# Graph attention of chunk 0 woven into the last attention iterations, and the first recurrence half step mixed with the last output products

## The chip, the cores and the metric

One core of one Trainium2 chip runs the whole program. The metric is the device time of one execution in microseconds (us). The engines are named as in the profile: PE (TensorE matmuls, with PEld its weight loads), DVE (VectorE), ACT (ScalarE), POOL (GpSimd) and SP (SyncE, which issues DMAs). Work passes between engines through semaphores; every engine runs its own instructions in program order.

## The reference

Four blocks follow each other on x of shape (128, 64, 256), each applied to h = relu(layernorm(x)) and added to x. The adjacency matrix (64 x 64) is the same for all 128 graphs.

```python
# block 0: masked attention, 8 heads of 32;  block 1 the same, then o + layernorm(o)*gamma + beta
scores = einsum('bqhd,bkhd->bhqk', q, k) / sqrt(HD);  attn = softmax(scores masked by adj)
out = einsum('bhqk,bkhd->bqhd', attn, v) @ Wo + bo
# block 2: graph attention
h = x @ W
e = leaky_relu(h@a1 [:, :, None] + h@a2 [:, None, :], 0.2) * mask
h_prime = einsum('bij,bjf->bif', softmax(e), h)
return elu(h_prime + beta * h)
# block 3: gated recurrence, T = 3 steps (the first factors of av are the adjacency products)
for _ in range(T):
    a_in = a_out = adj @ h;  av = concat([a_in, a_out])
    z = sigmoid(av@w3 + h@u3);  r = sigmoid(av@w4 + h@u3)
    hv = tanh(av@w5 + (r*h)@u5);  h = (1-z)*h + z*hv
```

## The kernel before, in words

x stays in SBUF for the whole program: 64 tiles of 128 rows, worked on as 16 chunks of 4 tiles (512 rows, 8 graphs). PSUM is two groups of four banks: `ring` and `scores` (also called `high`).

The two attention blocks are one software pipeline of 32 steps (T = 32; chunk c of block 0 is step c, chunk c of block 1 is step 16 + c). Iteration i does the scores and softmax of step i, the transposes and value products of step i-1, the output products of step i-2 and, in block 1, the normalisation of the output (steps i-3 and i-4), and it prepares q, k and v of step i+1. `iterations` runs the bodies: a few written out, a hardware loop of two bodies per turn, more written out, a second loop of five turns (iterations 20 to 29), and iteration 30. Iteration 31 and the drain of the pipeline are written out by hand after it, differently for each engine. Every float32 product is three products of split high and low parts (`product`, line 99), so PE runs most of the time on line 99.

Chunk 0 and chunk 1 of blocks 2 and 3 start in that hand written stretch. A chunk's graph attention is a serial chain over all engines: row statistics (DVE `rows_stats`), `norm` (POOL), `graph_normalise` (ACT), `graph_rows` (PE transposes), `graph_high` (ACT) and `graph_low` (DVE), four `graph_product` (PE) with `copy_hw` (ACT), `graph_s2` (PE), `graph_scores` (DVE), `g_shift` (POOL), `g_exponential` (ACT), `graph_attention` (DVE), `graph_attT` (PE), `copy_attT` (DVE), `graph_aggregate` (PE), and then `graph_out` on ACT and DVE, which adds to x. After it `recurrence_stats`, `norm`, `norm_rows` and `enter` bring the chunk into the recurrence.

The recurrence is a chain of half steps: two chunks are in flight, each half step does one step of one of them, and graph attention of the next two chunks runs inside them. `begin` is half step 0 of chunk 0; half step 1 (chunk 1) opens on DVE with r times h, line 1368, whose low part lets PE start the u5 products. From there on PE hardly waits. The order on each engine is that in which the code is written; there is no planner. One rule of the drain matters below: `o_normalise` of chunk c writes one of two buffers `o_n`, so it waits until `final_sum` of chunk c-2 has read it; `scale` (POOL) waits for it, and `final_sum` of c for `scale`.

## Time and profile before

| what | us |
|---|---|
| median of 3 runs | 1505.97 (1505.79 to 1506.27) |
| the profiled execution, its own time | 1503.79 |
| its span, first to last instruction | 1502.0 |
| PE, DVE, ACT, POOL busy in the span | 1464.7, 1246.0, 990.1, 536.0 |
| iterations 20 to 30 of the pipeline | about 369.6 to 562.6 in the span |
| iteration 31, drain and half step 0, up to PE's u5 products of half step 1 | 562.6 to 634.9 |

The busy share of PE is close to full over the whole program, except in the last of these stretches, where the granted clock is also lower for a time. PE's pipelined matmuls overlap, so PE counts as busy where it is only nearly so; start times of equal pieces of two iterations say more than the busy share.

### The profile page before, as it was taken

How to read it: one execution, taken by the hardware profiler on the slowest of the kernel's cores; microseconds unless marked ns; L12 is line 12 of the kernel's file. 1: busy time of each engine (PE TensorE's matmuls, PEld its weight loads, DVE VectorE, ACT ScalarE, POOL GpSimd, SP SyncE). 2: the span in 40 equal slices, each digit the busy share in tenths (PEclk: the TensorE clock that was granted, in tenths of full speed). 3: DMA queues.
4: the chain of work that ended last, by engine and by line, in shares of the span. 5: the costliest groups of instructions: out<-in, count | busy, mean ns of one | idle time of the engine just before them, and what ended most of it. 6: DMA issues, size and time to landing. Idle time of an engine off the chain costs nothing.

```text
span 1502.0 us, 45862 instructions
## 1 busy us (share of the span) xinstructions
PE 1464.7 (98%) x18922; PEld 1237.3 (82%) x18922; DVE 1246.0 (83%) x2518; ACT 990.1 (66%) x1795; POOL 536.0 (36%) x622
## 2 busy tenths in 40 slices
PE   8999999899999998799999999999999999999997
PEld 7898999799888887688888888888887887887886
DVE  4888877989999998888888888888888888888767
ACT  5767767567777776666666666666666666666564
POOL 3876776667888886411101101101111111111000
PEclk9999999999999999899999999999999999999999
DMA  8200000002333334100000000000000000000000
GB/s 268 87 2 0 0 0 2 16 17 45 60 68 68 58 57 59 29 1 1 29 1 2 30 1 1 30 1 1 30 1 1 30 1 1 29 2 1 29 2 28
DMA packets 36839, 40.89 MB, mean 27 GB/s; under 512 B 11872, under 2 KB 31840, under 8 KB 36704
## 3 DMA queue, kind: packets, MB, share of 16 engines
q0 software_dynamic: 4608, 16.78, 5.9%
q1 hardware_dynamic: 32096, 22.10, 4.9%
q8 instruction: 111, 1.82, 0.5%
q14 instruction: 24, 0.20, 0.0%
HBM read 13.71 MB, written 8.39 MB: 15 GB/s over the span
## 4 chain that ended last, share of the span: by engine, by line
PE 78%; DVE 11%; POOL 5%; issue 4%; ACT 1%; DMA 0%; POOLq 0%; DVEq 0%; SPq 0%; ACTq 0%
PE ring L99 34%; PE scores L99 28%; PE scores L1705 3%; DVE total L1040 2%; PE ring L1505 2%; PE ring L1774 2%; PE scores L1469 2%; POOL s L543 2%; PE ring L1545 1%; DVE stats L1012 1%; POOL rstd L534 1%; PE ring L1689 1%; PE ring L1846 1%; DVE oT_lo L1058 1%; PE ring L1647 1%
## 5 line engine op out<-in xcount | busy, mean ns | idle before, releaser
L543 POOL TENSOR_TENSOR s<-s,mx 128x512 f32<-128x512 f32 x128 | 138.3, 1103 | 56.0 <-DVE mx L1036 55.8
L549 POOL TENSOR_TENSOR s<-s,rtotal 128x512 f32<-128x512 f32 x128 | 131.8, 1067 | 31.8 <-DVE rtotal L1042 31.5
L613 POOL TENSOR_TENSOR r_var_eps<-r_mean_var,eps 128x4 f32<-128x4 f32 x16 | 8.1, 509 | 377.3 <-DVE r_mean_var L1207 377.3
L697 ACT ACTIVATE s<-s 128x512 f32<-128x512 f32 x128 | 77.9, 642 | 69.5 <-POOL s L543 69.5
L1370 DVE TENSOR_TENSOR rhp_lo<-r,rhp_hi 128x1024 fp32r<-128x1024 f32 x47 | 57.6, 1225 | 73.5 <-ACT rhp_hi L912 73.5
L1031 DVE SCALAR_TENSOR_TENSOR s<-scores,mask 128x512 f32<-128x512 f32 x128 | 87.1, 680 | 30.5 <-PE scores L1469 30.5
L877 ACT ACTIVATE r<-r,bias_half 128x512 f32<-128x512 f32 x96 | 64.3, 717 | 58.9 <-DVE r L1341 58.9
L931 ACT ACTIVATE hv<-scores,bias 128x512 f32<-128x512 f32 x94 | 64.7, 688 | 55.1 <-PE scores L99 55.1
L905 ACT ACTIVATE later_w<-ring 128x512 f32<-128x512 f32 x64 | 34.8, 596 | 99.1 <-PE ring L1774 99.1
L709 ACT ACTIVATE pT<-ring 128x512 f32<-128x512 f32 x128 | 66.1, 603 | 42.4 <-PE ring L1505 42.4
L1036 DVE TENSOR_REDUCE mx<-s 128x8 f32<-128x512 f32 x128 | 87.8, 686 | 4.4
L1332 DVE TENSOR_TENSOR agg_lo<-scores,agg_hi 128x512 fp32r<-128x512 f32 x96 | 61.8, 685 | 32.6 <-ACT agg_hi L870 32.2
L1040 DVE TENSOR_REDUCE total<-s 128x8 f32<-128x512 f32 x128 | 82.5, 645 | 0.0
L99 PE MATMUL ring<-agg_hi,w4T_hi 128*128 128x512 f32 x192 | 78.2, 407 | 2.3 <-DVE agg_lo L1332 2.3
L99 PE MATMUL scores<-rhp_hi,u5T_hi 128*128 128x512 f32 (+1 forms) x192 | 80.3, 418 | 0.0
L99 PE MATMUL scores<-agg_hi,w5T_hi 128*128 128x512 f32 (+1 forms) x192 | 78.3, 408 | 0.0
L99 PE MATMUL scores<-agg_hi,w3T_hi 128*128 128x512 f32 x192 | 77.2, 402 | 0.0
L613 POOL TENSOR_TENSOR g_var_eps<-g_mean_var,eps 128x4 f32<-128x4 f32 x16 | 8.3, 520 | 191.9 <-DVE g_mean_var L1207 191.9
L99 PE MATMUL scores<-agg_hi,w3T_lo 128*128 128x512 f32 x192 | 75.8, 395 | 0.0
L99 PE MATMUL scores<-agg_lo,w3T_hi 128*128 128x512 f32 x192 | 75.8, 395 | 0.0
L99 PE MATMUL ring<-agg_hi,w4T_lo 128*128 128x512 f32 x192 | 75.8, 395 | 0.0
L99 PE MATMUL ring<-agg_lo,w4T_hi 128*128 128x512 f32 x192 | 75.7, 394 | 0.0
(314 smaller groups left out, 5128.2 us busy)
## 6 DMA issues: line engine op xcount, KB each, us to landing
x<-beta_less_one POOLq DMA_DIRECT2D x16, 512.0 KB, 4.7
x<-o POOLq DMA_DIRECT2D x16, 512.0 KB, 6.6
out_x<-x SPq DMA_DIRECT2D x15, 512.0 KB, 2.9
x<-in_x SPq DMA_DIRECT2D x1, 6144.0 KB, 25.5
later_w<-in_L_gnn_w_w SPq DMA_DIRECT2D x3, 512.0 KB, 5.5
x<-in_x SPq DMA_DIRECT2D x2, 512.0 KB, 5.4
x<-in_x SPq DMA_DIRECT2D x1, 1024.0 KB, 7.0
stage<-in_L_gnn_w_qkv SPq DMA_DIRECT2D x3, 256.0 KB, 3.2
```

What stands on the lines that cost most here:

```text
L99: last = pe.matmul(out, s, m, start=(begins and n == 0), stop=(ends and n == len(terms) - 1))
L543: pool.tensor_tensor(sr, sr, mx[:, r, :].unsqueeze(2).to_broadcast([P, CT * 2, N]), ALU.subtract).then_inc(s_shifted, 1)
L549: pool.tensor_tensor(sr, sr, rtotal[:, r, :].unsqueeze(2).to_broadcast([P, CT * 2, N]), ALU.mult).then_inc(p_ready, 1)
L697: act.activation(s[:, par, r, :, :, :], s[:, par, r, :, :, :], ACT.Exp).then_inc(p_exp, 1)
L709: act.activation(pT[:, r, :, :].rearrange("p t q -> p (t q)"), ring[:, r, :], ACT.Copy).then_inc(pT_copied, 1)
L877: act.activation(r[:, m, :], r[:, m, :], ACT.Tanh, bias=bias_half[:, 1, m:m + 1], scale=0.5)\
L931: act.activation(hv[:, m, :], high[:, 2 + m, :], ACT.Tanh, bias=bias[:, 2, m:m + 1])\
L1031: dve.scalar_tensor_tensor(sr(par, r), scores[:, r, :].rearrange("p (a k) -> p a k", k=N), SCALE, masks[layer_of(i, lay)][:].unsqueeze(1). ...
L1036: dve.reduce_max(mx[:, r, :], sr(par, r), AX.X).then_inc(s_max, 1)
L1040: dve.reduce_sum(total[:, r, :], sr(par, r), AX.X).then_inc(p_total, 1)
L1332: dve.tensor_tensor(agg.lo[:].rearrange("p m (t g q) -> p g m t q", t=CT, g=2)[:, g], high[:, g, :].rearrange("p (m t q) -> p m t q", m=FT ...
L1370: dve.tensor_tensor(rhp.lo[:], r[:], f32(rhp.hi[:]), ALU.subtract).then_inc(rh_lo_ready, 1)
```

## The change

The second hardware loop is written out (iterations 20 to 30), since its bodies now differ. Chunk 0's graph attention is taken out of the hand written stretch and put into iterations 20 (WEAVE) to 30, a link or two in each, through functions `woven` and `woven_last` that each engine's body calls: statistics at the end of iteration 20, `norm` 21, `graph_normalise` 22, transposes and high and low parts 23, products 24 and 25, s2, sums and maximum 26, exponential 27, attention and its transposes 28, aggregation and the output to x 29, and the statistics for the recurrence 30. Chunk 1's statistics move one iteration earlier. The drain then holds chunk 1's graph attention, `enter` of chunk 0 and `begin`, in which the u3 products of chunk 0, the output products, the values, and the first adjacency products alternate. `o_normalise` and `final_sum` of the last chunks, and the last two `o_stats`, move into `begin`, behind the recurrence's own instructions. Chunk 0 gets buffers of its own; other buffers move to free the room (w_ext's place is taken by chunk 0's hw, then by its recurrence rows).

```diff
+    WEAVE = CHUNKS + 4
...
-            with eng.Fori(0, (CHUNKS - 6) // 2) as j:
-                body(j * 2 + CHUNKS + 4, 0, 1)
-                body(j * 2 + CHUNKS + 5, 1, 1)
-            body(T - 2, 0, 1)
+            for i in range(CHUNKS + 4, T - 1):
+                body(i, i % 2, 1)
...
                     if isinstance(i, int) and i == T - 2:
-                        norm(gn, 0, 0)
...
+                    if isinstance(i, int) and i == WEAVE + 1:
+                        norm(gn, 0, 0)
+                    if isinstance(i, int) and i == WEAVE + 6:
+                        g_shift(0)
...
                 scale(T - 1, 1, 1)
                 norms(T, 0, 1)
-                norm(rn, 0, 0)
-                g_shift(1)
                 scale(T, 0, 1)
+                norm(gn, 2, 0)
+                norm(rn, 1, 1)
+                o_to_x(T + 1, 1, 1)
                 norms(T + 1, 1, 1)
-                o_to_x(T + 1, 1, 1)
+                o_to_x(T + 2, 0, 1)
                 norms(T + 2, 0, 1)
-                o_to_x(T + 2, 0, 1)
-                norm(rn, 1, 1)
                 scale(T + 1, 1, 1)
                 scale(T + 2, 0, 1)
-                group(0)
+                norm(gn, 3, 1)
+                g_shift(2)
+                norm(rn, 2, 0)
+                g_shift(3)
+                norm(rn, 3, 1)
                 with pool.Fori(1, GROUPS - 1) as g:
...
+                def woven(i):
+                    if i == WEAVE + 3:
+                        graph_high(0, high)
+                    if i == WEAVE + 4:
+                        copy_hw(0, 0, high, 2)
+                        copy_hw(0, 1, high, 2)
+                    if i == WEAVE + 5:
+                        copy_hw(0, 2, high, 2)
+                        copy_hw(0, 3, high, 2)
+                    if i == WEAVE + 9:
+                        graph_read(0, high, 2)
+                def woven_last(i):
+                    if i == WEAVE + 2:
+                        graph_normalise(0, 0)
+                    if i == WEAVE + 7:
+                        g_exponential(0)
+                    if i == WEAVE + 9:
+                        graph_exp(0)
...
                 def begin(s):
                     for m in range(FT):
                         act.wait_ge(hu_ready, m + 1)
-                        act.activation(hu[:, m, :], ring[:, 2 + m, :], ACT.Copy).then_inc(hu_copied, 1)
-                    graph_read(1, ring, 0)
+                        act.activation(hu[:, m, :], high[:, m, :], ACT.Copy).then_inc(hu_copied, 1)
+                    g_exponential(1)
+                    o_normalise(T - 1, 1, 1)
+                    o_high(T - 1)
                     agg_high(0)
-                    graph_exp(1)
-                    o_normalise(T + 1, 1, 1)
-                    o_normalise(T + 2, 0, 1)
+                    graph_out(1, high, 2)
+                    o_normalise(T, 0, 1)
                     act.wait_ge(b_ready, 5)
                     r_tanh(0)
                     norm_rows(rn, r_hn[1], 1, 1)
                     enter(1, 1)
                     graph_normalise(2, 0)
+                    o_normalise(T + 1, 1, 1)
+                    o_normalise(T + 2, 0, 1)
...
                 act.wait_ge(xT_ready, T * FT)
-                graph_normalise(0, 0)
+                graph_normalise(1, 1)
                 copy_pT(T - 1)
-                o_normalise(T - 1, 1, 1)
-                graph_high(0, high)
+                norm_rows(rn, r_hn_first, 0, 0)
+                graph_high(1, high)
                 for q in range(R - 1):
                     exponential(T - 1, 1, q)
                 o_high(T - 2)
                 exponential(T - 1, 1, R - 1)
-                for t in range(CT):
-                    copy_hw(0, t, high, 2)
-                graph_normalise(1, 1)
+                copy_hw(1, 0, high, 2)
+                copy_hw(1, 1, high, 2)
+                enter(0, 0, high, 0)
+                copy_hw(1, 2, high, 2)
+                copy_hw(1, 3, high, 2)
                 copy_pT(T)
-                graph_high(1, high)
-                g_exponential(0)
-                o_high(T - 1)
-                copy_hw(1, 0, high, 0, hw_next)
-                copy_hw(1, 1, high, 0, hw_next)
-                graph_out(0, high, 2)
-                copy_hw(1, 2, high, 0, hw_next)
-                copy_hw(1, 3, high, 0, hw_next)
-                o_normalise(T, 0, 1)
-                norm_rows(rn, r_hn[0], 0, 0)
-                g_exponential(1)
-                enter(0, 0, high)
                 halves(act, half)
...
+                def woven(i):
+                    if i == WEAVE + 3:
+                        graph_low(0, high)
+                    if i == WEAVE + 6:
+                        graph_sum(0, high, 0)
+                    if i == WEAVE + 8:
+                        dve.wait_ge(beta_ident_ready, 1)
+                        copy_attT(0, high, 0)
+                    if i == WEAVE + 9:
+                        graph_positive(0, high, 2)
+                def woven_last(i):
+                    if i == WEAVE:
+                        dve.tensor_scalar(beta_ident[:], ident[:], g_beta[:, 0:1], None, ALU.mult)\
+                            .then_inc(beta_ident_ready, 1)
+                        rows_stats(gn, 0, x_final)
+                    if i == WEAVE + 6:
+                        graph_leaky(0)
+                    if i == WEAVE + 7:
+                        dve.memset(first_rows.att[:], 0.0).then_inc(first_att_cleared, 1)
+                    if i == WEAVE + 9:
+                        graph_negative(0)
+                    if i == WEAVE + 10:
+                        recurrence_stats(0)
...
                     if isinstance(i, int) and i == T - 2:
-                        rows_stats(gn, 0, x_final)
+                        rows_stats(gn, 1, x_final)
...
+                    if isinstance(i, int) and i == WEAVE + 8:
+                        graph_attention(0)
...
                 def begin(s):
-                    graph_positive(1, ring, 0)
+                    rows_stats(gn, 2)
+                    graph_positive(1, high, 2)
                     agg_low(0)
                     graph_negative(1)
                     recurrence_stats(1)
+                    take_first(T + 1, 1, 1)
+                    take_out(T - 1, 1, 1, 1)
                     r_sum(0)
+                    o_stats(T, 0, 1)
                     z_sum(0)
-                    rows_stats(gn, 2)
+                    dve.wait_ge(o_stats_ready, CHUNKS - 1)
+                    o_stats(T + 1, 1, 1)
+                    enter(1, 1)
+                    final_sum(T, 0, 1)
+                    final_sum(T + 1, 1, 1)
                     final_sum(T + 2, 0, 1)
-                    enter(1, 1)
...
-                rows_stats(gn, 1, x_final)
                 for q in range(3):
...
                 mask_and_max(T - 1, 1, 3, 1)
...
-                dve.tensor_scalar(beta_ident[:], ident[:], g_beta[:, 0:1], None, ALU.mult).then_inc(beta_ident_ready, 1)
-                graph_scores(0, high, 2)
+                enter(0, 0, high, 0)
+                graph_scores(1, high, 2)
                 final_sum(T - 1, 1, 1)
                 o_stats(T - 1, 1, 1)
                 dve.wait_ge(att_cleared, 1)
-                graph_attention(0)
-                graph_low(1, high)
-                dve.wait_ge(beta_ident_ready, 1)
-                copy_attT(0, high, 2)
+                graph_attention(1)
                 take_first(T, 0, 1)
                 take_out(T - 2, 1, 0, 1)
+                copy_attT(1, high, 2)
                 o_low(T - 1)
-                graph_out(0, high, 2)
-                recurrence_stats(0)
-                graph_scores(1, high, 0, hw_next)
-                o_stats(T, 0, 1)
-                take_first(T + 1, 1, 1)
-                take_out(T - 1, 1, 1, 1)
-                graph_attention(1)
...
+                def woven(i):
+                    if i == WEAVE + 3:
+                        pe.wait_ge(s_masked, i * R + 2)
+                        graph_rows(0, high)
+                    if i == WEAVE + 4:
+                        pe.wait_ge(gw_lo_ready, 1)
+                        pe.wait_ge(s_masked, (i + 1) * R)
+                        graph_product(0, 0, high, 2)
+                        graph_product(0, 1, high, 2)
+                    if i == WEAVE + 5:
+                        pe.wait_ge(s_masked, (i + 1) * R)
+                        graph_product(0, 2, high, 2)
+                        graph_product(0, 3, high, 2)
+                    if i == WEAVE + 6:
+                        pe.wait_ge(s_masked, i * R + 2)
+                        graph_s2(0, high, 0)
+                    if i == WEAVE + 8:
+                        pe.wait_ge(s_masked, i * R + 1)
+                        graph_attT(0, high, 0)
+                    if i == WEAVE + 9:
+                        pe.wait_ge(s_masked, (i + 1) * R)
+                        graph_aggregate(0, high, 2)
...
                 def begin(s):
                     pe.wait_ge(h0_lo_ready, FT)
-                    pe.wait_ge(x_done, T * 2)
                     for m in range(FT):
-                        product(pe, ring[:, 2 + m, :], columns(wT["u3"], m), moving(hp[0])).then_inc(hu_ready, 1)
-                    graph_aggregate(1, ring, 0, hw_next)
-                    pe.wait_ge(e_sum, 2)
-                    pe.wait_ge(hw_copied, 2 * FT)
+                        product(pe, high[:, m, :], columns(wT["u3"], m), moving(hp[0])).then_inc(hu_ready, 1)
+                    o_products(T, 1)
+                    graph_attT(1, high, 2)
+                    values(T, 0)
+                    pe.wait_ge(hu_copied, FT)
                     pe.wait_ge(adj_loaded, 32)
-                    adjacency(r_hn[0])
+                    adjacency(r_hn_first)
+                    graph_aggregate(1, high, 2)
+                    o_products(T + 1, 1)
                     pe.wait_ge(agg_lo_ready, FT)
-                    pe.wait_ge(x_plus_pos, 4)
                     for m in range(FT):
                         product(pe, ring[:, m, :], columns(wT["w4"], m), moving(agg)).then_inc(r_ready, 1)
                     for m in range(FT):
                         product(pe, high[:, m, :], columns(wT["w3"], m), moving(agg)).then_inc(z_ready, 1)
+                    pe.wait_ge(x_done, T * 2)
+                    enter(1, r_hn[1])
+                    pe.wait_ge(x_plus_pos, 4)
                     for m in range(FT):
                         product(pe, high[:, 2 + m, :], columns(wT["w5"], m), moving(agg), ends=False)
-                    pe.wait_ge(hu_copied, FT)
-                    enter(1, 1)
...
-                graph_rows(0, high)
+                graph_rows(1, high)
                 o_half(T - 1, 1, 1)
                 values(T - 1, 1)
-                pe.wait_ge(g_hT_lo_ready, FT)
-                pe.wait_ge(gw_lo_ready, 1)
                 pe.wait_ge(s_masked, T * R)
-                for t in range(CT):
-                    wait(pe, hw_copied, t // 2)
-                    graph_product(0, t, high, 2)
-                graph_s2(0, high, 2)
+                pe.wait_ge(g_hT_lo_ready, 2 * FT)
+                graph_product(1, 0, high, 2)
+                graph_product(1, 1, high, 2)
+                enter(0, r_hn_first, high, 0)
+                pe.wait_ge(hw_copied, FT + 1)
+                graph_product(1, 2, high, 2)
+                graph_product(1, 3, high, 2)
+                graph_s2(1, high, 2)
                 p_transposes(T, 0)
-                graph_rows(1, high)
-                o_products(T, 1)
-                values(T, 0)
-                graph_attT(0, high, 2)
-                pe.wait_ge(g_hT_lo_ready, 2 * FT)
-                graph_product(1, 0, high, 0)
-                graph_product(1, 1, high, 0)
-                graph_aggregate(0, high, 2)
-                pe.wait_ge(hw_copied, FT + 1)
-                graph_product(1, 2, high, 0)
-                graph_product(1, 3, high, 0)
-                graph_s2(1, high, 0, hw_next)
-                o_products(T + 1, 1)
-                pe.wait_ge(x_plus_pos, 2)
-                enter(0, 0, high)
-                graph_attT(1, ring, 0)
                 halves(pe, half)
```

Three places of the order follow. First DVE in iteration 28, between the second output copy (L1089, L1051 before) and the softmax sums (L1078, L1040). In every iteration before, and in iteration 21 of the change, there stands:

```order
L1051 TENSOR_TENSOR o<-ring,out_bias_93 128x512
L1058 TENSOR_TENSOR oT_lo<-ring,oT_hi 128x4x2x64
```

and in iteration 28 of the change:

```order
L1089 TENSOR_TENSOR o<-ring,out_bias_93 128x512
L1316 TENSOR_REDUCE g_total<-g_e 128x4
L1318 RECIPROCAL g_rtotal<-g_total 128x4
L1325 TENSOR_TENSOR g_att<-g_e,g_rtotal 64x4x64 x2
L1096 TENSOR_TENSOR oT_lo<-ring,oT_hi 128x4x2x64 x2
```

The four attention instructions now stand ahead of the low part of the output, and PE's transposes of g_att stand ahead of that iteration's q, k and v products. Second, ACT around `begin`, before (hw_next is chunk 1's hw, later_w the negative part of the graph output):

```order
L849 ACTIVATE hp_a_hi<-scores 128x512
L850 ACTIVATE h_a<-scores 128x512
L855 ACTIVATE hu<-ring 128x512 x2
L835 ACTIVATE later_w<-ring 128x2x256 x2
L870 ACTIVATE agg_hi<-scores 128x8x64 x2
L840 ACTIVATE later_w<-later_w 128x1024
L720 ACTIVATE o_n<-o,shift_by,rstd 128x256 x8
L877 ACTIVATE r<-r,bias_half 128x512 x2
L809 ACTIVATE r_hn_b<-x,r_shift_by,r_rstd 128x256 x4
```

In the change the normalisations of the last two chunks stand behind everything else of `begin`, ahead of the high part of r times h (waits shown):

```order
L853 ACTIVATE g_hn<-x,g_shift_by,g_rstd 128x256 [waits g_xT_ready,g_norm_ready]
L853 ACTIVATE g_hn<-x,g_shift_by,g_rstd 128x256 x3
L740 ACTIVATE o_n<-o,shift_by,rstd 128x256 [waits x_final,rstd_ready]
L740 ACTIVATE o_n<-o,shift_by,rstd 128x256 x3
L740 ACTIVATE o_n<-o,shift_by,rstd 128x256 [waits x_final,rstd_ready]
L740 ACTIVATE o_n<-o,shift_by,rstd 128x256 x3
L960 ACTIVATE rhp_hi<-r 128x1024 [waits x_plus_beta,x_plus_o,rh_done]
```

Third, DVE at the end of half step 0. Before, two of the three last `final_sum` were done ahead of `begin`, and one stands here:

```order
L1207 BN_AGGR g_mean_var<-g_stats 128x2 x4
L1085 TENSOR_TENSOR x<-x,o_n 128x1024
L1276 TENSOR_TENSOR hp_b_lo<-ring,hp_b_hi 128x512 x2
L1368 SCALAR_TENSOR_TENSOR r<-r,h_a 128x1024
L1370 TENSOR_TENSOR rhp_lo<-r,rhp_hi 128x1024
```

and in the change all three stand between chunk 1's entry and r times h:

```order
L1055 BN_AGGR mean_var<-stats 128x2 x4
L1356 TENSOR_TENSOR hp_b_lo<-ring,hp_b_hi 128x512 x2
L1123 TENSOR_TENSOR x<-x,o_n 128x1024 x3
L1455 SCALAR_TENSOR_TENSOR r<-r,h_a 128x1024
L1457 TENSOR_TENSOR rhp_lo<-r,rhp_hi 128x1024
```

## Rows read from the trace of the kernel before

**Rows 1.** Windows: length, then busy us (count) of PE, PEld, DVE, ACT, POOL, clock, DMA.

```profile
369.60:562.60 193.00, 192.87 (x3877) 170.47 (x3876) 179.32 (x449) 144.81 (x282) 161.22 (x170) 1.00 0.32 61
562.60:634.90 72.30, 56.64 (x838) 47.54 (x837) 61.85 (x138) 47.11 (x93) 41.00 (x54) 0.88 0.31 46
```

**Rows 2.** Timeline of PE: start, duration; scores, iterations 12, 13, 18, 19, 21, 31; two graph products.

```profile
223.43 1.59 PE L1469 MATMUL scores<-kT,qT 32*64 32x64 f32 x128
240.48 1.59 PE L1469 MATMUL scores<-kT,qT 32*64 32x64 f32 x128
...
334.45 1.59 PE L1469 MATMUL scores<-kT,qT 32*64 32x64 f32 x128
352.46 1.59 PE L1469 MATMUL scores<-kT,qT 32*64 32x64 f32 x128
359.58 1.49 PE L1545 MATMUL ring<-pT,v 64*32 64x64 f32 x128
...
386.67 1.60 PE L1469 MATMUL scores<-kT,qT 32*64 32x64 f32 x128
...
562.58 1.59 PE L1469 MATMUL scores<-kT,qT 32*64 32x64 f32 x128
...
572.05 0.39 PE L99 MATMUL scores<-g_w_hi,g_hT_hi 128*128 128x258 f32 x1
...
573.47 0.28 PE L99 MATMUL scores<-g_w_hi,g_hT_lo 128*128 128x258 f32 x1
```

**Rows 3.** Timeline of DVE in iteration 21 (in brackets the idle time before).

```profile
388.99 0.28 DVE L1007 BATCH_NORM_AGGREGATE mean_var<-stats 128x2 f32<-128x6 f32 x3
...
397.75 1.29 DVE L1058 TENSOR_TENSOR oT_lo<-ring,oT_hi 128x512 fp32r<-128x512 f32 x2 [0.83 <-ACT oT_hi L728]
```

**Rows 4.** Timeline of POOL and ACT in iteration 21.

```profile
397.40 2.50 POOL L575 TENSOR_TENSOR o_n<-o_n,gamma 128x1024 f32<-128x1024 f32 x1
...
391.78 2.08 ACT L720 ACTIVATE o_n<-o,shift_by,rstd 128x256 f32<-128x256 f32 x4
```

**Rows 5.** Timeline of DVE, pieces of the drain.

```profile
545.99 1.39 DVE L1202 BATCH_NORM_STATS2 g_stats<-x 128x6 f32<-128x256 f32 x4
...
577.16 1.80 DVE L1427 TENSOR_SCALAR beta_ident<-ident,g_beta 128x128 f32<-128x128 f32 x1
578.88 0.85 DVE L1225 TENSOR_TENSOR e<-scores,hw 64x256 f32<-64x256 f32 x2
...
581.01 1.22 DVE L1085 TENSOR_TENSOR x<-x,o_n 128x1024 f32<-128x1024 f32 x1
...
584.61 2.89 DVE L1245 TENSOR_TENSOR att<-e,g_rtotal 64x256 f32<-64x256 f32 x2
...
604.98 0.85 DVE L1245 TENSOR_TENSOR att<-e,g_rtotal 64x256 f32<-64x256 f32 x2
```

**Rows 6.** Timeline of POOL beside them.

```profile
583.79 2.99 POOL L575 TENSOR_TENSOR o_n<-o_n,gamma 128x1024 f32<-128x1024 f32 x1
```

**Rows 7.** PE behind two waits, and windows with the clock (columns as rows 1).

```profile
587.56 1.12 PE L1678 MATMUL scores<-ident,att 128*128 128x128 f32 x4 [2.80 <-DVE att L1245]
603.21 1.06 PE L1647 MATMUL scores<-ident,r_hn_a 128*128 128x128 f32 x8 [3.05 <-ACT r_hn_a L809]
...
585.00:595.00 10.00, 7.24 (x41) 5.50 (x42) 7.41 (x10) 2.83 (x7) 3.78 (x5) 0.66 0.46 88
605.00:615.00 10.00, 7.97 (x96) 5.90 (x96) 7.87 (x18) 3.91 (x8) 4.32 (x8) 0.69 0.28 54
```

**Rows 8.** DVE at both ends of the transition, PE where it ends.

```profile
565.10 0.66 DVE L1031 SCALAR_TENSOR_TENSOR s<-scores,mask 128x512 f32<-128x512 f32 x1
...
628.24 1.21 DVE L1368 SCALAR_TENSOR_TENSOR r<-r,h_a 128x1024 f32<-128x1024 f32 x1
632.60 1.22 DVE L1370 TENSOR_TENSOR rhp_lo<-r,rhp_hi 128x1024 fp32r<-128x1024 f32 x1 [3.15 <-ACT rhp_hi L912]
...
634.86 0.50 PE L99 MATMUL scores<-rhp_hi,u5T_hi 128*128 128x512 f32 x1
```

More of the change, by code:

```diff
@@ new lines, in network, with __init__ @@
+        adjT = sb("adjT", [P, P], F32, start["out_bias0"] + 512)
+        at_later = start["later_w"]
+        class GraphRows:
+            def __init__(self, tag, hn, hT, hw, e, attT):
+                self.hn = sb(f"{tag}_hn", [P, CT, D], F32, hn)
+                self.hT = Parts(plan, f"{tag}_hT", [P, FT, CW], hT)
+                self.hw = sb(f"{tag}_hw", [P, CT, WX], F32, hw)
+                self.e = sb(f"{tag}_e", [P, CT, N], F32, e)
+                self.e_lrelu = sb(f"{tag}_e_lrelu", [P, CT, N], F32, e + 1024)
+                self.att = sb(f"{tag}_att", [P, CT, 2, N], F32, e + 2048)
+                self.attT = sb(f"{tag}_attT", [P, CT, P], F32, attT)
@@ L1242, in graph_attention @@
                     wait(dve, attT_ready, c)
+                    if isinstance(c, int) and c == 0:
+                        dve.wait_ge(first_att_cleared, 1)
                     for g in range(2):
                         rows = slice(g * N, (g + 1) * N)
-                        last = dve.tensor_tensor(att[rows, :, g, :], e[rows, :, :],
+                        last = dve.tensor_tensor(to.att[rows, :, g, :], to.e[rows, :, :],
                                                  g_rtotal[rows, :].unsqueeze(2).to_broadcast([N, CT, N]), ALU.mult)
@@ L1558, in weight_transposes, with moving @@
                     last.then_inc(wT_ready, 1)
+                def moving(parts_):
+                    return [pair(parts_, slice(None), k, slice(None)) for k in range(FT)]
+                def woven(i):
[20 more added lines that the diff above has]
+                        graph_aggregate(0, high, 2)
                 def later_weights(i):
@@ L1639, in body @@
                             rows_product(hT, own["v"], 2 + g, g, v_ready)
-                def moving(parts_):
-                    return [pair(parts_, slice(None), k, slice(None)) for k in range(FT)]
                 def transposes(rows, psum, bank, signal):
@@ L1809, in half @@
                     if s.enters is not None:
-                        enter(s.enters, s.other)
+                        enter(s.enters, r_hn[s.other])
                     if s.graph_a is not None:
```

112 lines of the change are left out of this document (63 added, 49 removed).

## The prediction, made before the changed kernel was run

> **What bounds the kernel now.** I read the windows first. From iteration 20 to 30 PE is busy 192.87 of 193.00 us and DVE 179.32; in the 72.3 us after it PE falls to 56.64, DVE is still busy 61.85, and the granted clock is 0.88 [rows 1]. So the stretch that is emptied is the one with free time, and the one that is filled looks full. How full, the start of equal pieces tells better. Scores follow each other by 17.05 us in block 0 (223.43 to 240.48), and by (562.58 - 386.67) / 10 = 17.59 us in iterations 21 to 30 [rows 2]. PE's own work fills the 17.05: iteration 18, which has eight more transposes (1.06 us, as the 603.21 row of [rows 7]), took 18.01, 0.96 more [rows 2]. In block 1 something else adds 0.54 per iteration. In iteration 21 that is a chain on DVE: its only idle time between the statistics at 388.99 and the sums is 0.83 us ahead of oT_lo, waiting for ACT [rows 3]. So from 21 to 30 DVE sets the period, PE follows with 0.54 us of slack, and whatever DVE gets extra is paid nearly whole. In the drain the order is a chain over all engines: PE waits 2.80 us for the attention and 3.05 us for the recurrence's rows [rows 7], and DVE 3.15 us for the high part of r times h [rows 8].
>
> Written out bodies and looped ones have the same periods in [rows 2] (iterations 12 in the loop, 17.05; 18, with its transposes, the same plus their time), so I cost the unrolling at nothing.
>
> **A. What is added to iterations 20 to 30.** DVE, by iteration: 20, statistics 1.39 + 0.28 [rows 3, 5] and beta_ident, a quarter of a 128x512 pass of 0.66 [rows 8], 0.2 (in the drain it took 1.80 [rows 5]): 1.9. 23, low parts, two 128x512: 1.2. 26, sums, leaky, mask, maximum, 578.88 to 581.01 [rows 5]: 2.1. 27, a memset, 0.4 as an estimate under one 128x512 pass. 28, two attention passes 0.85, total and reciprocal 0.6, copy of attT 0.6: 2.1. 29, positive and negative part, 1.2 each: 2.4. Together 10.1. In 30 the recurrence's statistics come in, and chunk 1's at the head of the drain go: even. The 0.83 of idle time ahead of oT_lo [rows 3] takes one link in, the attention of 28: 10.1 - 0.8 = 9.3.
>
> Then the stalls that the links cause:
> - Iterations 24 and 25: two graph products each, 12 matmuls from 572.05 to 573.47, 1.42 us, ahead of q, k and v [rows 2]. Over a slack of 0.54 that is 0.9 twice if PE carries none over, nothing if DVE's own additions cover it. Between 0 and 1.7 I take 0.8. Iteration 22's `graph_normalise` (2.1 on ACT, as o_n at 391.78 [rows 4]) stands at the end of ACT's iteration, 0.2.
> - Iteration 28, PE. The transposes of g_att stand before q, k, v. In iteration 19 PE is through the values at 359.58 + 1.49, 8.6 us after its scores began [rows 2]. DVE comes to the attention where oT_lo stood in iteration 21, at 397.75, 11.1 us after the scores at 386.67, less 0.83 [rows 2, 3], and needs 1.5: 11.8. So PE idles about 3 us where it never idled, of which 0.54 is slack and a part comes back, since DVE itself is later by 2.1: 1.1, bounds 0 and 2.4.
> - Iteration 28, lock. POOL starts its scale at 397.40 for 2.50 us [rows 4], and the attention would start about there. In the drain the same two attention passes took 2.89 us at 584.61 beside such a scale (583.79 to 586.78), and 0.85 at 604.98 without [rows 5, 6]. Cost 0 or 2.0; I take 1.1.
> - Iteration 28, clock. Idle times of 2.80 and 3.05 us on PE are followed by windows at a mean granted clock of 0.66 and 0.69 over 10 us [rows 7], so by 6.8 and 6.2 us at the 1.2 GHz level. Then PE does in 6.8 us what it does in 3.4. Between 0 and 3.4 I take 1.2.
> - Iteration 29: the negative part waits for ACT's exp, which is written behind the copies of v. 0 to 2, I take 1.5, since these copies come last in ACT's iteration and are late already from 28.
> Stalls: 0.8 + 0.2 + 1.1 + 1.1 + 1.2 + 1.5 = 5.9. A = 15.2.
>
> The Trainium skill, "SBUF — State Buffer", section "SBUF: two separate sides", says that DVE and GpSimd share a port pair under an exclusive lock: who starts first keeps it for its whole instruction. The two attention passes above agree (2.89 beside the scale, 0.85 alone). By that rule the lock costs 28 either the whole rest of the scale or nothing, decided by 0.1 us. The sum keeps the middle.
>
> **B. What the transition gives back.** Before, DVE goes from its first mask pass at 565.10 to r times h at 628.24, and PE's u5 products start at 634.86 [rows 8]. The head of that, up to the end of the sums at 577.16, where beta_ident stands [rows 5], stays as it is. Behind it DVE now has: sixteen passes over 128x1024 or two halves of it (enter twice, final_sum four times, two output copies twice, oT_lo, positive, negative, agg_low, r_sum, z_sum, r times h, rhp_lo) at 1.25 from 1.22 and 1.29 [rows 3, 5] = 20.0; five statistics at 1.7 = 8.5; one scores link 2.1, attention 1.5, attT 0.6 = 4.2. Work: 32.7. Waits on that path: exponential 0.5, output copies behind their normalisation 0.5, oT_hi 1.1, chunk 1's entry 0.5, high part of r times h 1.0. And a new one, by the order: o_normalise of the last chunk waits for final_sum of the last but two, and that now stands behind chunk 1's entry. Behind it come ACT 2.08 and POOL 2.50 [rows 4], while DVE has 1.2 of its own: 3.8 with the signals. Waits: 7.4. So u5 would start at 577.2 + 32.7 + 7.4 = 617.3 instead of 634.9: B = 17.6. Bounds: if r times h alone is counted, it goes from 628.2 to 613.8, 14.4; if the new wait were absent, 21.4. The 2.80 and 3.05 us idle times and the 3.15 one are in this gain.
>
> **C. What is late next.** In its place PE idles while DVE does the final sums, and the clock may fall at the start of the half steps: 0 to 3.4 as above, I take 1.3. ACT and DVE come into the half steps behind PE: 0.8, bounds 0 and 1.7.
>
> **Sum.** 15.2 - 17.6 + 2.1 = -0.3 on the profiled execution's 1503.79 (span 1502.0), 1503.5. The median of the runs, 1505.97, stands 2.2 above that execution: forecast 1505.7.
>
> **Rivals.**
> 1. The links are absorbed. The attention starts before POOL's scale, PE's idle time in 28 stays far below those of [rows 7], and products and exp fall into slack: the 5.9 of stalls go. 1505.7 - 5.9 = 1499.8. For it: DVE is delayed by each of its own links, which gives PE and ACT as much slack. Against: in 28 the wait of PE follows from the order, not from a guess on size.
> 2. Slower, by the attention link of iteration 28. POOL holds DVE for its whole scale (2.0 instead of 1.1), PE waits some 5 instead of 3 us ahead of q, k, v (3.0 instead of 1.1), the clock falls to 1.2 GHz for a full 6.8 us (3.4 instead of 1.2): +5.0, 1510.7. It decides from the point where DVE reaches the attention behind the start of the scale, 10.7 us after the scores. For it: 11.1 - 0.8 = 10.3 against 10.7 is close, and 28 comes after iterations in which DVE was delayed and POOL was not. Against: POOL too follows DVE's statistics.
> 3. B doesn't come: values and output products of the drain hold `begin`, and u5 moves only by what r times h does, 14.4: 1508.9. It lies within the forecast's own range and is counted there.
>
> **How the numbers follow.** A measurement of this kernel tells about 0.2%, 3.0 us, from no change: 1503.0 to 1509.0. The forecast has 0.42, with its own range 1502 to 1509.5 (0.32 of it same, 0.05 each side), rival 1 0.33 (all faster), rival 2 0.25 (0.23 slower, 0.02 same). Faster 0.05 + 0.33 = 0.38, same 0.34, slower 0.28. The range over all goes down to 1496.5 (rival 1 with 3.3 more, less than the whole new wait of 3.8) and up to 1512.0.
>
> **What would show it.** Right: scores of 21 to 30 some 10 to 15 us further apart in sum, most of it at 26, 28 and 29; in 28 PE idle about 3 us for att ahead of its transposes and a window below 1.00 behind it; u5 some 52 us after DVE's first mask pass of iteration 31 instead of 69.8; DVE idle near 3.8 ahead of the last final_sum. Rival 1: PE never idle over 1 us in 28 and the clock 1.00. Rival 2: the attention passes at 2.9 us beside L575's pass and two windows at a lower clock. Wrong altogether: periods of 21 to 30 that grow by less than half of DVE's added work, or a wait ahead of `begin` that isn't in the list.

## The result, and the profile after

| | before | after |
|---|---|---|
| median of 5 runs, us | 1505.79 (1504.26 to 1506.27) | 1512.82 (1511.37 to 1514.23) |
| profiled execution / its span | 1503.79 / 1502.0 | 1512.27 / 1510.5 |

Ratio 1.0049, 95% interval 1.0039 to 1.0060: slower by 0.5%, 7.0 us. The forecast was no change (1505.7, range to 1512.0). Three marks divide the two spans: the scores of iteration 21, those of iteration 31, and the first u5 product of half step 1.

| stretch, us | before | after | difference | forecast |
|---|---|---|---|---|
| scores of 21 to scores of 31 | 175.9 | 193.8 | +17.9 | +15.2 |
| scores of 31 to u5 | 72.3 | 60.8 | -11.5 | -17.6 |
| u5 to the end | 867.2 | 869.6 | +2.4 | +2.1 |

(The start up to iteration 21 makes up the rest, -0.4.) The marks in the PE timeline after, which answer to [rows 2, 8]:

```profile
386.30 1.59 PE L1541 MATMUL scores<-kT,qT 32*64 32x64 f32 x128
...
542.39 1.60 PE L1541 MATMUL scores<-kT,qT 32*64 32x64 f32 x128
...
580.11 1.59 PE L1541 MATMUL scores<-kT,qT 32*64 32x64 f32 x128
...
640.90 0.79 PE L99 MATMUL scores<-rhp_hi,u5T_hi 128*128 128x512 f32 x1 [6.24 <-DVE rhp_lo L1457]
```

The starts of all scores from iteration 20 on, subtracted from each other, give the length of iterations 20 to 30: before 17.1, 17.5, 17.7, 17.5, 17.8, 17.5, 17.7, 17.6, 17.6, 17.5, 17.4; after 17.1, 19.5, 17.7, 18.2, 19.7, 18.6, 17.6, 18.6, **26.2**, 18.1, 19.6. One iteration, 28, carries 8.6 of the 17.9. Its DVE, POOL and PE rows, and the window with the clock (columns as [rows 1]), against [rows 5 to 7]:

```profile
526.95 0.41 DVE L1316 TENSOR_REDUCE g_total<-g_e 128x4 f32<-128x256 f32 x1
...
527.61 3.08 DVE L1325 TENSOR_TENSOR g_att<-g_e,g_rtotal 64x256 f32<-64x256 f32 x2
```

```profile
527.52 2.46 POOL L589 TENSOR_TENSOR o_n<-o_n,gamma 128x1024 f32<-128x1024 f32 x1
```

```profile
530.84 1.09 PE L1780 MATMUL scores<-ident,g_att 128*128 128x128 f32 x4 [5.20 <-DVE g_att L1325]
```

```profile
527.00:537.00 10.00, 6.16 (x17) 5.07 (x18) 9.75 (x20) 2.44 (x6) 7.02 (x6) 0.66 0.37 70
```

POOL's scale began 0.09 us ahead of the two attention passes; they took 3.08 us, PE stood idle for 5.20, and the clock was at 1.2 GHz for about 6.8 of the next 10 us. This is the second rival of the prediction, in its passes (2.9), its wait of PE (some 5) and its 6.8 us at the lower clock. The passes start 0.09 us behind the scale in all six executions profiled with this order (`after`, `filled_wait`, `adjacency_first`, `sums_later`, `pad_start`, `pad_loop`), and take 3.08 to 3.12 us in each.

In the transition three waits matter. PE, in chunk 0's adjacency products:

```profile
604.65 0.81 PE L1808 MATMUL scores<-adjT,r_hn_first 64*64 64x64 f32 x40
609.53 0.92 PE L1808 MATMUL scores<-adjT,r_hn_first 64*64 64x64 f32 x24 [4.06 <-issue]
```

64 matmuls of one loop, without a semaphore between them, stop after 40 for 4.06 us. "issue" means that nothing the profile shows held them. And DVE and POOL (the first row's 4.49 us is what that stop does to DVE), where u5 is late:

```profile
612.88 1.29 DVE L1340 SCALAR_TENSOR_TENSOR x<-scores,x 128x512 f32<-128x512 f32 x2 [4.49 <-ACT later_w L880]
...
634.01 3.35 DVE L1123 TENSOR_TENSOR x<-x,o_n 128x1024 f32<-128x1024 f32 x1 [3.81 <-POOL o_n L589]
637.28 1.21 DVE L1455 SCALAR_TENSOR_TENSOR r<-r,h_a 128x1024 f32<-128x1024 f32 x1
```

```profile
627.78 0.93 POOL L582 DMA_DIRECT2D x<-o  x1 [2.50 <-DMA x<-o]
...
631.60 4.67 POOL L589 TENSOR_TENSOR o_n<-o_n,gamma 128x1024 f32<-128x1024 f32 x2
```

The new wait is 3.81 us, as the prediction had it (3.8). But the pass behind it takes 3.35 us instead of 1.22 [rows 5], since POOL's next scale runs beside it.

Is anything loading while PE stands? Of two windows of the DMA view, 593.0 to 605.4 and 605.4 to 609.5 (packets, MB, share), the first has no packet of queue q8, the second has one:

```profile
q8 instruction: 1, 0.02, 1.7%
q14 instruction: 1, 0.01, 0.5%
```

By its own record this q8 packet (16 KB of instructions) starts at 606.9 and takes 1.14 us; the one before it started at 592.0. That gave the theory for the experiments: PE had run out of its stored program.

The DMA record also shows what was under way until then. The window 601.0 to 606.8 holds this of queue q0, and nothing of q8:

```profile
q0 software_dynamic: 287, 1.05, 96.4%
```

It is the data of two transfers that POOL issues, x<-beta_less_one and x<-o, 512 KB each, 288 packets from 601.06 to 606.92, and the q8 packet starts with the last of them.

### The profile page after: what moved, and what is told of

The parts are those of the page before. It is cut to its first block, busy times and chain, and to the rows that moved or that the text cites. A ratio compares the mean times of both kernels' runs of the same rounds, so it can differ in the third digit from the quotient of the medians.

```text
span 1510.5 us, 45252 instructions
## 1 busy us (share of the span) xinstructions
PE 1461.8 (97%) x18922; PEld 1239.1 (82%) x18922; DVE 1246.9 (83%) x2519; ACT 991.0 (66%) x1795; POOL 535.5 (35%) x622
## 4 chain that ended last, share of the span: by engine, by line
PE 79%; DVE 10%; POOL 5%; ACT 2%; issue 2%; DMA 1%; DVEq 0%; POOLq 0%
PE ring L99 35%; PE scores L99 28%; PE scores L1808 3%; PE ring L1581 2%; PE scores L1541 2%; PE ring L1879 2%; POOL s L557 1%; PE ring L1621 1%; DVE total L1078 1%; DVE s L1069 1%; PE ring L1792 1%; DVE hT_lo L1166 1%; DVE stats L1040 1%; PE ring L1951 1%; ACT pT L729 1%
## 5 line engine op out<-in xcount | busy, mean ns | idle before, releaser
L1069 DVE SCALAR_TENSOR_TENSOR s<-scores,mask 128x512 f32<-128x512 f32 x128 | 87.2, 682 | 34.8 <-PE scores L1541 34.8
L953 ACT ACTIVATE later_w<-ring 128x512 f32<-128x512 f32 x64 | 34.8, 596 | 100.4 <-PE ring L1879 100.4
L1412 DVE TENSOR_TENSOR agg_lo<-scores,agg_hi 128x512 fp32r<-128x512 f32 x96 | 61.8, 685 | 32.7 <-ACT agg_hi L918 32.3
L1078 DVE TENSOR_REDUCE total<-s 128x8 f32<-128x512 f32 x128 | 82.6, 645 | 0.0
L99 PE MATMUL scores<-rhp_lo,u5T_hi 128*128 128x512 f32 (+1 forms) x192 | 76.4, 398 | 0.0
L99 PE MATMUL scores<-rhp_hi,u5T_lo 128*128 128x512 f32 (+1 forms) x192 | 76.2, 397 | 0.0
L99 PE MATMUL scores<-agg_lo,w5T_hi 128*128 128x512 f32 (+1 forms) x192 | 76.0, 396 | 0.0
```

The costliest lines, as they stand in the source:

```text
L99: last = pe.matmul(out, s, m, start=(begins and n == 0), stop=(ends and n == len(terms) - 1))
L1069: dve.scalar_tensor_tensor(sr(par, r), scores[:, r, :].rearrange("p (a k) -> p a k", k=N), SCALE, masks[layer_of(i, lay)][:].unsqueeze(1). ...
L1078: dve.reduce_sum(total[:, r, :], sr(par, r), AX.X).then_inc(p_total, 1)
L1412: dve.tensor_tensor(agg.lo[:].rearrange("p m (t g q) -> p g m t q", t=CT, g=2)[:, g], high[:, g, :].rearrange("p (m t q) -> p m t q", m=FT ...
```

## The experiments

All change the changed kernel, but for the first. "u5" is the time from the scores of iteration 31 to the first u5 product (after: 60.8).

**Written out bodies alone.** `unroll` is the kernel before with this edit:

```diff
-            with eng.Fori(0, (CHUNKS - 6) // 2) as j:
-                body(j * 2 + CHUNKS + 4, 0, 1)
-                body(j * 2 + CHUNKS + 5, 1, 1)
-            body(T - 2, 0, 1)
+            for i in range(CHUNKS + 4, T - 1):
+                body(i, i % 2, 1)
```

> The kernel before with iterations 20 to 30 written out and nothing else changed. If written out bodies cost nothing: every period of iterations 21 to 30 within 0.1 us of before (17.4 to 17.8), time within 1 us of before. Rival, that the longer program has to be fetched and PE stops for it: periods longer by 0.3 us or more each, or single stops of PE of some us that no semaphore explains, 3 to 8 us in all.

Measured: 1505.29 against 1505.08, ratio 1.0003 (0.9994 to 1.0012). Iterations 21 to 30 took 17.4 to 17.8 us, no stop. Unrolling costs nothing in these iterations; the rival falls there.

**The attention link earlier.**

```diff
 # ACT: g_exponential(0) from woven_last (WEAVE + 7) to woven (WEAVE + 7)
 # DVE
                     if i == WEAVE + 6:
                         graph_leaky(0)
-                    if i == WEAVE + 7:
                         dve.memset(first_rows.att[:], 0.0).then_inc(first_att_cleared, 1)
+                    if i == WEAVE + 7:
+                        graph_attention(0)
...
-                    if isinstance(i, int) and i == WEAVE + 8:
-                        graph_attention(0)
```

> The changed kernel with the link of iteration 28 earlier: exponential in the middle of ACT's iteration 27, attention at the end of DVE's iteration 27 (memset in 26), PE's transposes where they were. If the place of the link is the cause (attention beside POOL's scale, PE waiting for it, clock): PE no longer idle ahead of the transposes, iteration 28 falls from 26.2 to about 18.5, 27 grows from 18.6 by about 1, the time falls by 6 to 7 us to about 1506. Rival, that DVE's added work is what costs and the wait only shows it: PE waits for something else in 27, 28 or 29 and the time falls by 2 us at most, to 1511.

Measured: 1507.78, ratio to before 1.0019 (1.0010 to 1.0028), so 5 of the 7 us come back. Iteration 28 took 19.3, 27 19.0, 29 19.2; the passes:

```profile
519.36 0.85 DVE L1324 TENSOR_TENSOR g_att<-g_e,g_rtotal 64x256 f32<-64x256 f32 x2
```

The place of the link is the cause. Of the 6.9 us won in 28, 1.5 went to 27 and 29, and 1.0 to 21 (0.5 of it came back in 22). The length of 21 goes with the granted clock. PE waits 1.9 to 2.0 us in it in every one of these kernels; in the six profiles with 20.4 to 20.6 us the clock falls behind that wait, in the five with 19.4 to 19.6 it doesn't. First `early_att`, then `after`:

```profile
395.00:405.00 10.00, 9.50 (x160) 7.98 (x161) 8.95 (x19) 7.67 (x16) 9.97 (x10) 0.83 0.57 107
```

```profile
395.00:405.00 10.00, 10.00 (x176) 8.30 (x176) 8.96 (x20) 7.98 (x16) 9.98 (x10) 1.00 0.57 107
```

Iteration 30 does the same in four of the profiles (20.6 instead of 19.6, `att_before_scale` among them). What decides between the two is not shown; in a single run it is 1 us either way.

**What holds the passes.**

```diff
+                    if isinstance(i, int) and i == WEAVE + 8:
+                        pool.wait_ge(att_ready, 1)
                     scale(i, par, lay)
```

> The changed kernel, but in iteration 28 POOL's scale waits until the attention is written. If POOL's scale held DVE: the two attention passes take 0.85 instead of 3.08 us, PE's idle time ahead of the transposes falls from 5.2 to about 3.0; the clock still falls (PE idle for 3 us was enough in the kernel before), so iteration 28 goes from 26.2 to about 24, the time down by 2. Rival, that most of iteration 28 is the clock, and an idle time of 3 us in the middle of the pipeline doesn't lower it: clock 1.00, iteration 28 near 21. Second rival, that the passes are slow by themselves: 3 us again and nothing changes.

Measured: 1508.6 (one run). DVE, then PE, then the window:

```profile
527.45 0.85 DVE L1327 TENSOR_TENSOR g_att<-g_e,g_rtotal 64x256 f32<-64x256 f32 x2
```

```profile
528.45 0.63 PE L1782 MATMUL scores<-ident,g_att 128*128 128x128 f32 x4 [2.97 <-DVE g_att L1327]
```

```profile
527.00:537.00 10.00, 8.55 (x37) 7.16 (x38) 9.61 (x28) 5.81 (x12) 6.91 (x6) 0.83 0.36 68
```

0.85 instead of 3.08 with the same start (11.4 us after the scores, 11.5 before): it was POOL's scale. PE still idles for 2.97 us by the order alone, as the prediction had it (about 3). Iteration 28: 22.9, 3.4 us less; the clock still falls, for about half as long.

**What the idle time costs in clock.**

```diff
                         pe.wait_ge(s_masked, i * R + 1)
+                        keep_clock(high[:, 0, :], 40)
                         graph_attT(0, high, 0)
```

> The changed kernel with 40 idle transposes (results never read) put on PE in iteration 28 between the values and the wait for the attention; they take 2 to 5 us of the 5.2 us of idle time. If the lower clock costs 3 us of iteration 28: clock 1.00 around it and iteration 28 about 23 instead of 26.2. Rival, that the clock falls all the same or is not what costs: 26 or more. It also moves every later instruction of PE 80 further: if the stop in begin belongs to a place of the instruction stream, it comes 80 instructions of the program earlier, at the end of the values; if it belongs to the adjacency products, it stays at them.

Measured: 1506.4 (one run). The window over the same 10 us:

```profile
527.00:537.00 10.00, 9.39 (x64) 8.37 (x65) 9.71 (x18) 4.15 (x8) 7.04 (x6) 1.00 0.52 99
```

Iteration 28 took 23.5, with the passes still slow (3.12): the lower clock cost 2.8 of its 26.2 (25.6 to 26.2 in the five profiles with the same order and no filling). And the stop of 4 us in `begin` was gone, u5 at 56.5, where the expectation had it at the end of the values or at the adjacency products. Two effects at once, so the next ones take the second apart. (The timing of iteration 28 is not what removed it: `early_att`, where 28 took 19.3, still stopped at the same adjacency product, for 4.04 us.)

**The stop: the work, or the place?**

```diff
-                    values(T, 0)
                     pe.wait_ge(hu_copied, FT)
                     pe.wait_ge(adj_loaded, 32)
                     adjacency(r_hn_first)
+                    values(T, 0)
```

> The changed kernel with chunk 0's adjacency products ahead of the values in begin. If PE stops where its instruction stream reaches a certain count, whatever stands there: the stop of 4 us comes again after the same number of matmuls, now within the values, and the adjacency products run without one, so that agg_hi comes some 4 us earlier but oT_hi later. Rival, that something about the adjacency products (their rows, adjT's landing) stops them: the stop is in them again, earlier.

Measured: 1512.3 (one run), no gain, and

```profile
604.62 1.16 PE L1808 MATMUL scores<-adjT,r_hn_first 64*64 64x64 f32 x64
605.71 1.28 PE L1621 MATMUL ring<-pT,v 64*32 64x64 f32 x104
610.86 0.43 PE L1621 MATMUL ring<-pT,v 64*32 64x64 f32 x24 [3.87 <-issue]
```

128 + 40 = 64 + 104 = 168: the stop comes after the same number of matmuls, in other work. (`three_cures`, below, has the aggregation's 16 ahead of the adjacency products and stops behind 24 of these: 128 + 16 + 24, again 168.)

**The place: executed or stored?**

```diff
-                keep_clock(high[:, 0, :], 48)
+                keep_clock(high[:, 0, :], 88)        # pad_start
...
+                with pe.Fori(0, 4):                  # pad_loop
+                    keep_clock(high[:, 0, :], 12)
```

> The changed kernel with 40 more idle transposes among the 48 that PE does at its very start: 80 instructions more ahead of everything, nothing changed near begin. filled_wait lost its stop; it had 80 more instructions and also another timing from iteration 28 on. If the stop belongs to places of the stored program: it goes here too (u5 at 56.5 instead of 60.8 after the scores of iteration 31), though the kernel starts some 3 to 5 us later. Rival, that the timing of iteration 28 made it go: the stop of 4 us stays at the same adjacency product and u5 at 60.8.

> The changed kernel with the 48 idle transposes at PE's start written as a loop of 4 turns of 12: some 70 stored instructions fewer, the same work. If the stop belongs to places of the stored program: it comes some 70 instructions later in the order of the work (behind the adjacency products, in the aggregation or the output products, where one instruction takes longer and less of it may show), or not at all. If it belongs to the count of what was executed or to the work itself, it stays at the same adjacency product, 4.1 us.

Measured: `pad_start` 1515.5, `pad_loop` 1517.8 (one run each; both lose time in early iterations: iterations 1 and 2 of `pad_start` took 19.9 and 18.7 us, after 16.9 and 17.1). `pad_start` in `begin`:

```profile
612.40 1.16 PE L1808 MATMUL scores<-adjT,r_hn_first 64*64 64x64 f32 x64
613.39 1.05 PE L1792 MATMUL scores<-g_hw,g_attT 64*64 64x256 f32 x16
```

and `pad_loop`:

```profile
612.62 1.16 PE L1808 MATMUL scores<-adjT,r_hn_first 64*64 64x64 f32 x64
613.60 1.03 PE L1792 MATMUL scores<-g_hw,g_attT 64*64 64x256 f32 x10
617.51 1.12 PE L1792 MATMUL scores<-g_hw,g_attT 64*64 64x256 f32 x6 [2.89 <-issue]
```

80 stored instructions more, at the far end of the program: the stop is gone, u5 at 56.2. Some 70 fewer with the same work: it comes 24 + 10 matmuls later (with their weight loads 68 instructions), 2.89 us. So where it comes belongs to a place of the stored program. The Trainium skill, "Runtime: NRT & Kernel Launch", section "Instruction fetch mechanics", says that instructions come in blocks of 16 KiB (256 of them) that the sequencer fetches itself, and calls the cost of a block's edge mostly hidden. The trace agrees on the size of the packets; it does not agree here on the cost, 4.06 us at one place. Ahead of it stand 168 matmuls of 64x64 and smaller tiles within 2.2 us (603.24 to 605.46). That the place is such an edge is argued from the packet's time, not shown.

Whether PE stops there, and how long, goes with the data transfers of `begin`. In all seven profiles with the stop (`after`, `early_att`, `att_before_scale`, `adjacency_first`, `three_cures`, `sums_later`, `pad_loop`) the q8 packet starts within 0.01 us of the last packet of the 1.05 MB in queue q0, and PE goes on 2.4 to 2.7 us behind that start, whether it had stood for 4.06 or for 2.89 us. In the four without it (`filled_wait`, `pad_start`, `cures_a`, `cures_b`) a q8 packet comes 0.3 to 1.9 us behind the first of those data packets. `filled_wait`, 599.5 to 605.0, the data again from 599.6:

```profile
q0 software_dynamic: 278, 1.02, 99.0%
q8 instruction: 1, 0.02, 1.1%
```

So the likeliest reading is that instructions asked for early enough arrive beside the data, and that those asked for a little later wait for all of it: the place decides when they are asked for, the transfer how long they take. This rests on the times of the packets; no run moved the transfers.

**Three cures together.** The earlier link, the aggregation ahead of the adjacency products, and

```diff
# DVE begin, and half step 1 behind rhp.lo
-                    final_sum(T + 2, 0, 1)
...
+                        final_sum(T + 2, 0, 1)
                         final_sum(T + 3, 1, 1)
```

> The changed kernel with the earlier attention link, with graph_aggregate of chunk 1 put between the values and the adjacency products on PE in begin, and with the final_sum that waits for the last but one scale moved behind r times h and its low part. Each cause by itself: 6.5 for iteration 28, about 4 for PE's stop in the adjacency products, 4.7 for the final_sum (wait 3.8, pass beside a scale 3.35 instead of 1.2, less ACT's own end at 633.8). If they add up: 15 us less than the changed kernel, 1497.5. Rival, that the drain is bound by another chain (DVE's own work): the stop goes and half step 1 starts at most 4 us earlier, 1502.

Measured: 1505.84, ratio to before 1.0003 (0.9994 to 1.0012); u5 at 57.8. They don't add up: PE's stop was still there, shorter by what stood ahead of it (its end is tied to the packet, which starts at 601.68):

```profile
604.28 1.35 PE L1808 MATMUL scores<-adjT,r_hn_first 64*64 64x64 f32 x40 [2.97 <-issue]
```

and behind r times h DVE now waited 4.27 us for the high part, which ACT does behind two normalisations, the second of which waits 1.31 us for POOL, and POOL 2.49 for the landing of x<-o. My rival had the size (1502) nearer, but not its reason.

**The last sums further back.** The last two `final_sum` behind `graph_stats` of half step 1, POOL's last scale behind rhp.lo, `norms(T + 2)` ahead of `o_to_x(T + 2)`.

> The changed kernel with the last two final_sum behind the statistics of half step 1, POOL's last scale behind the low part of r times h, and POOL's norms of the last chunk ahead of its DMA. If the final_sum behind the last but one scale and its lock make up the late u5: u5 58.4 us after the first mask pass goes to about 52 (the sum of the prediction without the PE stop would give 48). Rival, found with three_cures (57.8 from the scores of iteration 31, was 60.8): ACT's normalisation behind POOL's wait for a DMA holds the high part anyway, and only 3 to 4 us come back.

Measured: 1513.2 (one run). PE's stop was still there (4.06), yet u5 came 5.4 us earlier (55.4), and half step 1 took 25.7 instead of 22.0 us: two sums now stood between agg_lo and the update of h, ACT waited 5.1 us for h, and PE for g_hw:

```profile
652.11 1.12 PE L1774 MATMUL ring<-ident,g_hw 64*64 64x64 f32 x16 [3.12 <-ACT g_hw L868]
```

Won and given back, as neither expectation had it.

**Towards a better kernel.** Both of the next two kernels have the earlier link, the final_sum of T + 2 behind rhp.lo, and 40 small transposes in iteration 30, where PE waited 2.1 us anyway, which move `begin` by 80 stored instructions:

```diff
+                        if isinstance(hT_split, int) and hT_split == T * FT and t % 2 == 1:
+                            for _ in range(40):
+                                pe.transpose(ring[0:N, bank, D:D + N], ident[0:N, 0:N], ident[0:N, 0:N])
                         if hT_split is not None and t % 2 == 1:
                             pe.wait_ge(hT_lo_ready, hT_split)
```

> The changed kernel with the earlier attention link, with 40 small idle transposes (64x64) on PE in iteration 30 in the 2 us in which it waits for hT_lo, which move begin by 80 stored instructions, and the final_sum of the last but one chunk behind the low part of r times h. three_cures took 1505.8 with PE's stop of 3.0 us still in it. If the stop is a matter of stored places: it goes, u5 comes at 53 to 54 after the scores of iteration 31 (57.8 there) and the time is 1501 to 1502.5, faster than before by 0.2 to 0.3%. Rival, that PE isn't what the end of begin waits for once the final_sum is moved (ACT's normalisation behind POOL's wait for a DMA is): u5 at 56 to 57, 1504 to 1505.

Measured: 1502.16, ratio to before 0.9981 (0.9972 to 0.9990); u5 at 53.9. `cures_b` adds POOL's edits of the last experiment and moves only final_sum(T + 3) behind the statistics.

> As cures_a, and also: POOL's norms of the last chunk ahead of its DMA, its last scale behind the low part of r times h, and the last final_sum behind the statistics of half step 1. If the DMA wait and the scale beside the low part (2.60 us there, in three_cures) hold u5: another 2 us, 1499 to 1500.5. Rival, seen in sums_later (u5 5.4 earlier, next half step 3.7 longer): what is won at u5 is lost in half step 1, and the time is that of cures_a or 1 us above.

Measured: 1498.7 (1498.35 to 1500.17), ratio 0.9959 (0.9945 to 0.9972): faster than both kernels. u5 came at 50.7, and half step 1 took 23.3 (22.5 in `cures_a`). Its adjacency products run through, and PE no longer waits long for the low part:

```profile
601.47 1.16 PE L1813 MATMUL scores<-adjT,r_hn_first 64*64 64x64 f32 x64 [0.55 <-issue]
```

```profile
626.98 0.50 PE L99 MATMUL scores<-rhp_hi,u5T_hi 128*128 128x512 f32 x1 [0.79 <-DVE rhp_lo L1457]
```

Its 21 to 30 cost 12.5 us more than before, its transition gives 21.6 back, and half step 1 takes 3.6 of that.

## Why the prediction was wrong

The profiled execution took 1512.27 where the sum had 1503.5, 8.8 more. Of this B is 6.1, A 2.7, and the rest cancels to nothing. Two steps failed: the waits in B, and iteration 28 in A.

- **What bounds it, A's work.** Right. DVE's added work was paid nearly whole: in `cures_b`, without the stalls of 28, the ten iterations cost 12.5 us for 10.1 of DVE work. Iterations 23 to 25 cost 3.7 more where 2.0 was forecast; 26, 27, 29 and 30 cost 3.6 together where 6.4 was. (A link at the end of an iteration is paid in the next: 29 and 30 cost 0.6 and 2.2, together 2.8 for the 3.9 of positive part, negative part and exp.) These 2.8 us less are luck: without them the forecast would have missed by more.
- **Iteration 28: the step that failed in A.** The mechanisms were all named, the sizes were the middles of ranges near whose ends the truth lay. It cost 8.6, the forecast had 4.7 (2.1 - 0.8 of work, stalls 3.4), the rival 5.0 more than that. (The rival's total, 1510.7, is near the measured one only by half for its own reason: it had 1.1 too much here, and B as the forecast had it.) The lock: the sum took 1.1 of 2.0; the runs showed 2.2 (3.08 against 0.85). It was not a matter of chance: the step compared the scale's start with DVE's arrival at the link, and forgot that total and reciprocal, 0.66 us, run ahead of the two passes. With them DVE comes behind the scale, 10.9 against 10.7 in the prediction's own numbers, and in all six executions. PE's idle time by the order was right (3 forecast, 2.97 alone). The clock: 1.2 taken, 2.8 measured.
- **B: the step that failed is "waits on that path".** It gave 7.4 us; in DVE's rows from the end of the sums (594.70) to u5 they add up to 11.4, and the rest is 34.8 where 32.7 us of work stood. Two things were missing. PE's stop of 4.06 us was in no view of the kernel before, and it cost 4.3 to 4.6 at u5 (60.8, and 56.5 or 56.2 where it was gone). The final_sum was costed at 1.2 and took 3.35, the same lock that I had weighed for 28 and did not look for here, where POOL has two scales in a row and DVE's pass is released by the first: 2.1, read from the rows, since no run took it away alone. Together at least 6.4, against the 6.1 us by which B fell short. The new wait itself was right (3.81).
- **C.** +2.4 against 2.1, by window 640 to 650 at a clock of 0.70.
- **Unrolling at nothing.** Right for the iterations (1.0003). The cost of a stored program came elsewhere: at one place of `begin`, beside a data transfer, and it goes or moves when anything ahead of it grows. Rival 3 had the direction (14.4 for B, it was 11.5) without the mechanism.
- **The chances.** "Slower" had 0.28. The lock in 28 was no coin toss once total and reciprocal are counted, so the second rival deserved more than 0.25, and with the new wait and two scales in a row a lock in B should have stood in the sum.

What stays open: whether the instruction packet really waits for the data transfers of `begin`, which a run with these transfers moved would show, and why the clock falls behind a wait of 1.9 us in iteration 21 in some kernels and not in others.

## What to carry to other kernels

When a link is put between two engines' streams, compare starts instruction by instruction, not link by link: 0.66 us of total and reciprocal put DVE's passes behind the start of POOL's scale, and the price was paid three times (the pass, the engine that waits for it, the clock behind its idle time). Put a link an iteration before it is needed; slack that costs nothing there saved 5 us. After moving code, look for stops that the profile gives to "issue", and at the DMA queues beside them: an instruction packet that starts as a data transfer ends is a lead. This one could be cured by shifting the stored program, and an experiment that changes instruction counts can move such a stop without meaning to.

## What was not expected of the hardware

A run of matmuls without waits stopped for 4.06 us at a place of the stored program, beside a 16 KB instruction packet that started 1.4 us into the stop, with the last packet of 1.05 MB of data; 80 idle instructions hundreds of microseconds ahead removed it (u5 60.8 to 56.2), 70 fewer moved it by 34 matmuls. Forty idle transposes in a wait of 5.2 us kept the granted clock at 1.00 over a window that otherwise had 0.66, and made the iteration 2.8 us shorter. Behind a wait of 1.9 to 2.0 us the clock fell in six profiles and stayed in five, 20.5 against 19.5 us for the iteration.
